# Moving layer three's general pass behind the first two edge groups, and adding a block's two half sums in one instruction

## The chip, the cores and the metric

The kernel runs on one core of one Trainium2 chip. The metric is device time in microseconds (us) of one execution. TensorE (PE) multiplies, VectorE (DVE) and ScalarE (ACT) work elementwise, GpSimd (POOL) here mostly issues gathers (indirect DMAs, which fetch one row of a table for each partition), and SyncE (SP) issues plain DMAs. The engines run side by side, each through its own queue in the order of the program, and wait for each other by semaphores.

## The reference

Three graph layers on 6250 nodes with 128 features and E = 106250 edges, sorted by `dst`. The change lies in the last one alone:

```python
h_edge = jnp.concatenate([x[src], x[dst]], axis=-1)
m_ij = jax.nn.relu(h_edge @ W_interact + b_interact)
m_i = jax.ops.segment_sum(m_ij, src, num_segments=x.shape[0])
m_i = m_i / jnp.asarray(math.sqrt(AVG_DEGREE), dtype=x.dtype)
out = x + jax.nn.relu((x + m_i) @ W_update + b_update)
```

## The kernel before

Layers one and two take the time up to 874 us, where the first product of layer three (L1400) starts. Between them the kernel also sorts the edges by their source, for layer three.

Layer three starts with two products for each node, kept as tables: `a` (the part of `x[src]`, in SBUF as `a_kept`) and `b` (the part of `x[dst]` with the bias, stored to DRAM as `b_rows`). PE makes them in ten chunks (L1400); VectorE adds the bias to b (`b_part`, L2090 and L2093), GpSimd makes the low half of the b tiles that stay in SBUF (L892), and SyncE stores b to `b_rows` (L720).

Then come 50 blocks of 125 source nodes. The sorted edges of a block lie in 18 tiles of 128 edge slots, worked in six groups of three tiles, so there are 300 groups, `gi` from 0 to 299. For a group:

- VectorE makes one-hot matrices that pick rows (`prepare`, L2151, three groups ahead, one instruction for each tile whose b rows are picked by a product; for a block's first group also L2143, which makes those of all 18 tiles for the a rows; for two groups in six also `source_hot`, L2170).
- PE picks the a rows, and for 9 of the 18 tiles the b rows, into a PSUM bank (`edge_sum`, L1434 and L1443).
- For the other 9 tiles of a block GpSimd fetches the b rows from `b_rows` (`fetch`, L901, one gather for a tile, into a ring of nine group buffers that the program calls cells, cell_hi and cell_lo). A buffer is free again when VectorE has added it (semaphore `e_full`), nine groups earlier.
- VectorE adds the gathered rows in PSUM (`add_rows`, L2182), ScalarE takes the relu (L1120), VectorE makes its low half (`low_term`, L2190), and PE sums by source node (`source_sum`, L1454).

At a block's end the high and the low half of the sum lie side by side in PSUM, [125, 2 x 128]. `whole_sum` on VectorE copies the first half to SBUF (L2198) and then adds the second to it (L2200), and `turn_sum` on PE transposes the result (L1466). `whole_sum` for block b - 1 stands in group 4 of block b, behind that group's `prepare`, and directly ahead of `add_rows` of group 5.

The sort reserves a fixed number of slots for each block. A general pass takes care of inputs for which that isn't enough: in that case it goes over all edges tile by tile, in a loop whose trip count is in `trips`. For these inputs the trip counts are one, and the one trip adds zero. It still runs once: VectorE makes two node numbers (`g_node`, L2113, and `g_src`, L2114), GpSimd gathers one row of a and one of b (L918), VectorE adds, clips and scales them (L2117 to L2119), makes a one-hot (L2124), PE multiplies (L1416), and VectorE adds the result to `hT` (L2129). In VectorE's queue and in PE's it stands ahead of all 50 blocks. In GpSimd's it stands behind `fetch(0)` and `fetch(1)`, and GpSimd waits there for the store of `a_rows` (SP, L725) and for `g_idx`.

Of the kernel before, what the change touches and what calls it, by code (L numbers as in the profile page):

```python
# [6 lines left out]
def gnn_kernel(nc, x, src, dst, W_l0, W_r0, b0, W_l1, W_r1, b1, W_int, b_int, W_upd, b_upd, out):  # L7
# [5 lines left out]
    ALU = mybir.AluOpType  # L13
# [169 lines left out]
    with ctx:  # L183
# [404 lines left out]
        SOON = 2  # L588
        BUILT = 10
# [538 lines left out]
        def _(pe):  # L1128
# [283 lines left out]
            n_t, n_b = trips_of(pe)  # L1412
            with pe.Fori(0, n_t) as T:
                with pe.Fori(0, n_b) as b:
                    pe.wait_ge(g_onehot, T * NB + b + 1)
                    t.matmul(ps[:, 6, 0:BN], g_msg, g_hot, start=True, stop=True).then_inc(g_sum, 1)  # L1416
# [30 lines left out]
            def source_sum(gi):  # L1447
# [3 lines left out]
                if g == 0 and b > 1:  # L1451
                    pe.wait_ge(e_whole, 2 * (b - 1))
# [6 lines left out]
            def turn_sum(b):  # L1459
                pe.wait_ge(e_whole, 2 * b + 2)  # L1460
                if b:
                    pe.wait_ge(e_added, b)
                updated = sum(last < b for last in LAST_BLOCK)
                if updated:
                    pe.wait_ge(o_biased, updated)
                t.transpose(ps[:, 7, 2 * P:2 * P + BN], block_sum[0:BN, :], ident[0:BN, 0:BN]).then_inc(e_turned, 1)  # L1466
# [11 lines left out]
            for gi in range(NGR):  # L1478
# [3 lines left out]
                edge_sum(gi)  # L1482
                if g == 2 and b > 1:
                    turn_sum(b - 2)
# [11 lines left out]
        def _(dve):  # L1496
# [611 lines left out]
            n_t, n_b = trips_of(dve)  # L2108
            GENERAL = 3
            with dve.Fori(0, n_t) as T:  # L2110
                chain, n = chained(g_step, T * GENERAL)
                one = pairs[:, bass.ds(T + 1, 1), :].rearrange("p a k -> p (a k)")
                v.tensor_scalar(g_node[:, :], one, gate[:, 3:4], None, ALU.min).then_inc(g_idx, 1)  # L2113
                v.tensor_scalar(g_src[:, :], one[:, 0:1], 1.0, None, ALU.mult).then_inc(g_next, 1)  # L2114
                for k in range(2):
                    dve.wait_ge(g_rows[k], T * 16 + 16)
                chain(v.tensor_tensor(out=g_msg, in0=g_a, in1=g_b, op=ALU.add))  # L2117
                chain(v.tensor_scalar(g_msg, g_msg, 0.0, None, ALU.max))
                chain(v.tensor_scalar(g_msg, g_msg, gate[:, 1:2], None, ALU.mult))  # L2119
                assert n[0] == GENERAL  # L2120
                dve.sem_inc(s_past[1], 1)
                with dve.Fori(0, n_b) as b:
                    dve.wait_ge(g_next, T * (NB + 1) + b + 1)
                    v.tensor_scalar(g_hot, iota_w[:, 0:BN], g_src[:, 0:1], None, ALU.is_equal).then_inc(g_onehot, 1)  # L2124
                    dve.wait_ge(g_onehot, T * NB + b + 1)
                    v.tensor_scalar(g_src[:, :], g_src[:, :], -float(BN), None, ALU.add).then_inc(g_next, 1)
                    dve.wait_ge(g_sum, T * NB + b + 1)
                    to = hT[:, bass.ds(b * BN, BN)]
                    v.scalar_tensor_tensor(out=to, in0=ps[:, 6, 0:BN], scalar=settle[:, 0:1], in1=to,  # L2129
                                           op0=ALU.mult, op1=ALU.add).then_inc(g_added, 1)  # L2130
                    dve.wait_ge(g_added, T * NB + b + 1)
# [62 lines left out]
            def whole_sum(b):  # L2194
                dve.wait_ge(e_psum, (b + 1) * GB)
                if b:
                    dve.wait_ge(e_turned, b)
                v.tensor_copy(block_sum[0:BN, :], ps[0:BN, 4 + b % 2, 0:D]).then_inc(e_whole, 1)  # L2198
                dve.wait_ge(e_whole, 2 * b + 1)
                v.tensor_tensor(out=block_sum[0:BN, :], in0=block_sum[0:BN, :], in1=ps[0:BN, 4 + b % 2, D:2 * D],  # L2200
                                op=ALU.add).then_inc(e_whole, 1)
# [21 lines left out]
            AHEAD = 3  # L2223
# [4 lines left out]
            for gi in range(NGR):  # L2228
# [45 lines left out]
```

## Time and profile before

| | |
|---|---|
| median of three runs | 1581.64 us (1581.3 to 1582.77) |
| the profiled execution | 1582.7 us, its span 1580.9 us |
| busy in the span: PE, VectorE, ScalarE, GpSimd | 1343.8, 1323.1, 874.6, 968.7 us |
| from the first gather of layer three to the end of the span | 918.16 to 1580.9 us |
| gathers of layer three | 450 in L901, 2 in L918 |

The span runs from the first to the last instruction on the core; the time of an execution is a little more. Line numbers are those of the kernel before. A group of rows names line, engine, operation, and what was written from what. "x3" at a row's end is the number of instructions merged in it.

### The profile page before, as it was taken

How to read it: one execution, taken by the hardware profiler on the slowest of the kernel's cores; microseconds unless marked ns; L12 is line 12 of the kernel's file. 1: busy time of each engine (PE TensorE's matmuls, PEld its weight loads, DVE VectorE, ACT ScalarE, POOL GpSimd, SP SyncE). 2: the span in 40 equal slices, each digit the busy share in tenths (PEclk: the TensorE clock that was granted, in tenths of full speed). 3: DMA queues.
4: the chain of work that ended last, by engine and by line, in shares of the span. 5: the costliest groups of instructions: out<-in, count | busy, mean ns of one | idle time of the engine just before them, and what ended most of it. 6: DMA issues, size and time to landing. Idle time of an engine off the chain costs nothing.

```text
span 1580.9 us, 38635 instructions
## 1 busy us (share of the span) xinstructions
PE 1343.8 (85%) x14762; PEld 1138.4 (72%) x14762; DVE 1323.1 (84%) x3131; ACT 874.6 (55%) x1635; POOL 968.7 (61%) x940
## 2 busy tenths in 40 slices
PE   1623888999999988999998859989899999998987
PEld 1311566777777766777776759989898988888886
DVE  7968887999999845767776769989898988998987
ACT  2643676878778930110001637767666766666764
POOL 5263804777771007677750277777777787777775
PEclk9955899999999999999999879999999999999998
DMA  3003644656464238899984234444444444444442
GB/s 118 1 1 98 225 198 142 222 181 245 156 254 144 84 101 283 283 311 306 302 278 154 58 86 131 125 124 123 115 124 114 123 121 114 121 116 123 124 113 74
DMA packets 121777, 241.56 MB, mean 153 GB/s; under 512 B 20184, under 2 KB 74601, under 8 KB 121594
## 3 DMA queue, kind: packets, MB, share of 16 engines
q1 hardware_dynamic: 95179, 187.74, 35.3%
q0 software_dynamic: 24832, 50.78, 13.0%
q8 instruction: 118, 1.93, 0.5%
q10 hardware_dynamic: 1584, 0.59, 0.1%
q14 instruction: 64, 0.52, 0.1%
HBM read 169.09 MB, written 73.14 MB: 153 GB/s over the span
## 4 chain that ended last, share of the span: by engine, by line
PE 34%; DVE 29%; POOL 13%; DMA 9%; issue 9%; SPq 4%; DVEq 1%; ACT 1%; POOLq 0%
PE ps L1238 13%; POOL cells L901 6%; PE ps L1220 5%; DVE hot L1782 4%; PE ps L1443 4%; POOL cell_lo L901 4%; DMA cells<-b_rows,work 4%; POOL cell_hi L901 3%; PE ps L1209 3%; DMA cell_hi<-b_rows,work 3%; SPq L643 2%; DVE room L2151 2%; PE ps L1278 2%; DVE keys L1908 2%; DVE keys L1907 2%
## 5 line engine op out<-in xcount | busy, mean ns | idle before, releaser
L990 ACT ACTIVATE slab<-ps 128x980 f16<-128x980 f32 x256 | 321.6, 1277 | 116.9 <-PE ps L1209 102.2
L901 POOL DMA_INDIRECT cells<-b_rows,work x236 | 271.0, 1148 | 73.7 <-issue 65.5
L1443 PE MATMUL ps<-slab,room 125*128 125x128 f16 x3538 | 236.7, 221 | 20.2 <-DVE room L2151 19.8
L1220 PE MATMUL ps<-slab,room 128*128 128x320 f16 x1568 | 252.2, 301 | 0.1
L1443 PEld LDWEIGHTS ps<-slab,room 125*128 125x128 f16 x3538 | 208.1, 98 | 29.7 <-DVE room L2151 29.6
L1434 PE MATMUL ps<-inv,hot 125*128 125x128 f16 x1800 | 225.2, 221 | 3.7 <-DVE hot L2143 3.6
L1238 PE MATMUL ps<-slab,room 128*128 128x320 f16 x1568 | 227.3, 301 | 0.0
L1209 PE MATMUL ps<-hot 128*128 128x245 bf16 x1024 | 161.8, 283 | 48.7 <-DVE hot L1782 38.0
L865 POOL DMA_INDIRECT hot<-t_rows,pairs x160 | 165.5, 1034 | 55.6 <-issue 48.2
L1238 PEld LDWEIGHTS ps<-slab,room 128*128 128x128 f16 x1568 | 153.2, 98 | 59.8 <-issue 2.7
L1099 ACT ACTIVATE lnw<-iota_w,keys 128x126 f32<-128x126 f32 x600 | 193.9, 389 | 0.0
L1220 PEld LDWEIGHTS ps<-slab,room 128*128 128x128 f16 x1568 | 153.4, 98 | 47.8 <-issue 1.0
L1443 PE MATMUL ps<-slab 125*128 125x128 f16 x2676 | 181.7, 221 | 6.0 <-DVE slab L2151 5.7
L1782 DVE TENSOR_TENSOR hot<-iota_hi,cell_hi 128x984 bf16<-128x984 bf16 x256 | 170.2, 665 | 0.0
L1209 PEld LDWEIGHTS ps<-hot 128*128 128x128 bf16 x1024 | 108.1, 116 | 85.7 <-DVE hot L1782 51.7
L1443 PEld LDWEIGHTS ps<-slab 125*128 125x128 f16 x2676 | 158.3, 98 | 10.4 <-DVE slab L2151 9.8
L865 POOL DMA_INDIRECT tslot<-t_rows,pairs x80 | 95.1, 1189 | 98.8 <-PE ps L1278 67.1
L1434 PEld LDWEIGHTS ps<-inv,hot 125*128 125x128 f16 x1800 | 144.2, 98 | 10.6 <-DVE hot L2143 3.7
L901 POOL DMA_INDIRECT cell_lo<-b_rows,work x115 | 126.4, 1099 | 35.0 <-issue 31.7
L1907 DVE TENSOR_TENSOR keys<-keys 128x256 f32<-128x256 f32 (+1 forms) x212 | 111.9, 528 | 37.2 <-ACT keys L973 21.7
L1120 ACT ACTIVATE slab<-ps 128x384 f16<-128x384 f32 x200 | 95.8, 479 | 77.4 <-DVE ps L2182 74.5
L901 POOL DMA_INDIRECT cell_hi<-b_rows,work x99 | 113.4, 1145 | 30.2 <-issue 26.8
(367 smaller groups left out, 2413.2 us busy)
## 6 DMA issues: line engine op xcount, KB each, us to landing
slabs_d<-slab SPq DMA_DIRECT2D x14, 3920.0 KB, 13.7
slab<-slabs_d SPq DMA_DIRECT2D x98, 560.0 KB, 5.2
hot<-lane_d SPq DMA_DIRECT2D x50, 576.0 KB
inv<-inv_row SPq DMA_DIRECT2D x32, 160.0 KB, 6.5
keys<-up_d SPq DMA_DIRECT2D x25, 160.0 KB
room<-up_d SPq DMA_DIRECT2D x25, 160.0 KB
cells<-b_rows,work POOLq DMA_INDIRECT x236
t_rows<-room SPq DMA_DIRECT2D x1, 3200.0 KB, 13.7
```

What stands on the lines that cost most here:

```text
L865: p.indirect_dma_start(tail_rows[L][i % RT[L]], None, t_rows[L], bass.IndirectOffsetOnAxis(ap=pairs[:, t, 0:1], axis=0)).then_inc(e_gath[a ...
L901: p.indirect_dma_start(rows_g[gi % RS][:, j, :], None, b_rows, bass.IndirectOffsetOnAxis(ap=node_t[:, t:t + 1], axis=0)).then_inc(e_gath[g ...
L990: a.activation(slab[par][:, :, u * UB * BW:(u + 1) * UB * BW].rearrange("p h (k d) -> p k h d", k=UB), psum_unit(u).rearrange("p k (h d) - ...
L1099: last = a.activation(far[:, j, :], iota_w[:, 0:BE], ACT.Square, bias=lane_g[:, gi * GT + j:gi * GT + j + 1])
L1120: a.activation(msg[gi % 3][:, :, 0, :], ps[:, gi % 4, 0:GW].rearrange("p (j f) -> p j f", j=GT), ACT.Relu).then_inc(e_msg, 1)
L1209: last = t.matmul(to[:, k, :], lo[:, :, k], hi[:, k, 0:HB], start=True, stop=True)
L1220: last = t.matmul(ps[:, 4 + s % 2, 0:SC], table[:, h, term, :], slab[s % 2][:, h, :], start=k == 0, stop=k == HI * HALVES - 1)
L1238: last = t.matmul(ps[:, 4 + q % 2, 0:SC], table[:, h, term, :], slab[q % 2][:, h, :], start=k == 0, stop=k == HI * HALVES - 1)
L1434: last = t.matmul(to, lanes_of, a_terms[0:BN, b % 2, k, :], start=k == 0, stop=not picked and k == HALVES - 1)
L1443: last = t.matmul(to, end_hot[g // 3][0:BN, u:u + P], bt[0:BN, bt_at(tile, w), k, :], start=False, stop=w == w1 - 1 and k == HALVES - 1)
L1782: v.tensor_tensor(out=hot[:, u % 4, P * UB:(P + HB + 1) * UB].rearrange("p (k w t) -> p k w t", k=UB, t=2), in0=iota_hi[:, :].rearrange("p ...
L1907: v.tensor_tensor(out=new[0], in0=old[0], in1=old[1], op=ALU.max if down else ALU.min)
```

## The change

It makes two edits. The general pass keeps its place in GpSimd's and SyncE's queues. In VectorE's and PE's it moves into the loop over groups: on VectorE into gi = 1 (`GENERAL_AT`), behind `prepare(4)`; on PE behind `edge_sum(4)` (`GENERAL_AT + AHEAD`). The two node numbers of its first trip are made where the pass stood (`general_pair`), and those of the next trip at a trip's end. And `whole_sum` is one `tensor_reduce` over the two halves, which reads them with a step of 128 elements between the two addends.

```diff
@@ PE
-            n_t, n_b = trips_of(pe)
-            with pe.Fori(0, n_t) as T:
...
+            def general_edges():
+                n_t, n_b = trips_of(pe)
...
-                    pe.wait_ge(e_whole, 2 * (b - 1))
+                    pe.wait_ge(e_whole, b - 1)
...
-                pe.wait_ge(e_whole, 2 * b + 2)
+                pe.wait_ge(e_whole, b + 1)
...
                 edge_sum(gi)
+                if gi == GENERAL_AT + AHEAD:
+                    general_edges()
@@ VectorE
-            n_t, n_b = trips_of(dve)
-            GENERAL = 3
-            with dve.Fori(0, n_t) as T:
-                chain, n = chained(g_step, T * GENERAL)
-                one = pairs[:, bass.ds(T + 1, 1), :].rearrange("p a k -> p (a k)")
+            def general_pair(at):
+                one = pairs[:, at, :].rearrange("p a k -> p (a k)")
                 v.tensor_scalar(g_node[:, :], one, gate[:, 3:4], None, ALU.min).then_inc(g_idx, 1)
                 v.tensor_scalar(g_src[:, :], one[:, 0:1], 1.0, None, ALU.mult).then_inc(g_next, 1)
...
+            general_pair(slice(1, 2))
+
+            def general_edges():
+                n_t, n_b = trips_of(dve)
+                GENERAL = 3
+                with dve.Fori(0, n_t) as T:
+                    chain, n = chained(g_step, T * GENERAL)
+                    for k in range(2):
+                        dve.wait_ge(g_rows[k], T * 16 + 16)
+                    chain(v.tensor_tensor(out=g_msg, in0=g_a, in1=g_b, op=ALU.add))
...
+                    general_pair(bass.ds(T + 2, 1))
...
-                v.tensor_copy(block_sum[0:BN, :], ps[0:BN, 4 + b % 2, 0:D]).then_inc(e_whole, 1)
-                dve.wait_ge(e_whole, 2 * b + 1)
-                v.tensor_tensor(out=block_sum[0:BN, :], in0=block_sum[0:BN, :], in1=ps[0:BN, 4 + b % 2, D:2 * D],
-                                op=ALU.add).then_inc(e_whole, 1)
+                v.tensor_reduce(out=block_sum[0:BN, :], in_=ps[0:BN, 4 + b % 2, 0:2 * D].rearrange("p (k f) -> p f k", k=2),
+                                op=ALU.add, axis=AX.X).then_inc(e_whole, 1)
...
+                if gi == GENERAL_AT:
+                    general_edges()
```

In the order of VectorE's instructions the place is where the b part ends and the blocks start. Before, the pass (L2113 to L2129, with the loops' own steps) comes first, then the first block's preparation:

```order
L2113 TENSOR_SCALAR g_node<-pairs,gate 128x2
L2114 TENSOR_SCALAR g_src<-pairs 128x1
L2116 ISA
L2117 TENSOR_TENSOR scaled<-inv 128x128
...
L2129 SCALAR_TENSOR_TENSOR hT<-ps,settle,hT 128x125
...
L2160 TENSOR_TENSOR inv<-room,inv 125x128
L2143 TENSOR_SCALAR hot<-hot,lane_c 125x2304
```

After, line numbers are 10 or 11 higher. VectorE reaches the first block's preparation straight from the two node numbers, and the pass follows the preparation of the fifth group:

```order
L2115 TENSOR_SCALAR g_node<-pairs,gate 128x2
L2116 TENSOR_SCALAR g_src<-pairs 128x1
L2171 TENSOR_TENSOR inv<-room,inv 125x128
L2154 TENSOR_SCALAR hot<-hot,lane_c 125x2304
...
L2162 TENSOR_TENSOR slab<-keys,down_c 125x896
L505 TENSOR_LOAD trips
L505 ISA x2
...
L2127 TENSOR_TENSOR scaled<-inv 128x128
...
L2139 SCALAR_TENSOR_TENSOR hT<-ps,settle,hT 128x125
```

The gathered rows aren't waited for ahead of the first block any more. On PE the pass's product stood between the b part and the first group; after, it stands behind the picks of the fifth group (L1437 and L1446), and the loads of the trip counts stand there too:

```order
L1457 MATMUL ps<-slab,tslot 126x256 x3
L1437 MATMUL ps<-inv,hot 128x128 x2
L1446 MATMUL ps<-slab 128x128 x14
L1437 MATMUL ps<-inv,hot 128x128 x4
L505 TENSOR_LOAD trips
...
L1419 MATMUL ps<-scaled 128x125
```

GpSimd's, SyncE's and ScalarE's instructions and their order are the same in both kernels.

## Rows read from the trace of the kernel before

**Rows 1.** The page, part 4: shares of the chain that ended last, by engine

```profile
PE 34%; DVE 29%; POOL 13%; DMA 9%; issue 9%; SPq 4%; DVEq 1%; ACT 1%; POOLq 0%
```

**Rows 2.** Timeline of VectorE: start us, us, instruction, [idle before <-releaser]

```profile
914.77 1.32 DVE L2113 TENSOR_SCALAR g_node<-pairs,gate 128x2 int32 x1 [0.18 <-issue]
...
924.87 0.29 DVE L2117 TENSOR_TENSOR scaled<-inv 128x128 f32<-128x128 f32 x1 [8.74 <-DMA inv<-b_rows,g_node]
...
928.75 0.29 DVE L2160 TENSOR_TENSOR inv<-room,inv 125x128 f16<-125x128 f32 x1 [0.46 <-DVE hT L2129]
928.96 1.00 DVE L2143 TENSOR_SCALAR hot<-hot,lane_c 125x2304 f16<-125x2304 f16 x1
...
933.30 0.30 DVE L2182 TENSOR_TENSOR ps<-ps,cells 128x128 f32<-128x128 f32 x1 [0.82 <-PE ps L1434]
```

**Rows 3.** Timeline of TensorE

```profile
926.98 0.79 PE L1416 MATMUL ps<-scaled 128*128 128x125 f32 x2 [13.98 <-DVE scaled L2124]
```

**Rows 4.** Timeline of GpSimd

```profile
918.16 0.96 POOL L901 DMA_INDIRECT cells<-b_rows,work  x1 [2.11 <-DMA b_rows<-cells]
...
920.93 0.94 POOL L918 DMA_INDIRECT inv<-a_rows,g_node  x1 [0.56 <-issue]
...
923.43 0.94 POOL L901 DMA_INDIRECT cells<-b_rows,work  x1 [0.30 <-issue]
...
1567.62 0.94 POOL L901 DMA_INDIRECT cells<-b_rows,work  x1 [0.30 <-issue]
```

**Rows 5.** Waits of GpSimd, 917 to 1581 us: total us, times, longest

```profile
POOL cells L901 <- issue: 65.5, 215, 0.3
...
POOL cells L901 <- DVE ps L2182: 6.1, 20, 0.3
```

**Rows 6.** Waits of VectorE: first row 930 to 1000 us, the others 1000 to 1575 us

```profile
DVE ps L2182 <- PE ps L1434: 2.3, 2, 1.5
...
DVE ps L2182 <- DMA cells<-b_rows,work: 20.2, 23, 2.3
DVE ps L2182 <- DMA cell_hi<-b_rows,work: 19.8, 15, 3.6
DVE ps L2182 <- DMA cell_lo<-b_rows,work: 8.6, 8, 2.6
```

**Rows 7.** Stretches, L901 alone: length, POOL busy (x gathers), TensorE's granted clock, DMA

```profile
918.10:932.70 14.60, 9.08 (x9) 0.50 0.23 49
932.70:1007.20 74.50, 58.05 (x54) 0.98 0.46 121
1007.20:1478.20 471.00, 372.31 (x324) 0.99 0.44 120
1478.20:1556.20 78.00, 61.48 (x54) 0.98 0.44 120
```

**Rows 8.** Timelines of GpSimd (two rows) and VectorE (five) around one whole_sum

```profile
1230.52 1.56 POOL L901 DMA_INDIRECT cells<-b_rows,work  x1 [0.30 <-issue]
1232.39 0.94 POOL L901 DMA_INDIRECT cells<-b_rows,work  x1 [0.30 <-issue]
...
1230.12 1.15 DVE L2151 TENSOR_TENSOR room<-keys,up_c 125x896 f16<-125x896 f16 x2
1231.18 0.28 DVE L2198 COPY scaled<-ps 125x128 f32<-125x128 f32 x1
...
1231.71 0.42 DVE L2182 TENSOR_TENSOR ps<-ps,cell_lo 128x256 f32<-128x256 f32 x1
1232.04 0.55 DVE L2190 SCALAR_TENSOR_TENSOR work<-ps,work 128x384 f16<-128x384 f32 x1
1232.51 0.75 DVE L2151 TENSOR_TENSOR room<-keys,up_c 125x1152 f16<-125x1152 f16 x1
```

**Rows 9.** Timeline of VectorE: a dense reduce, its successor, a copy written with a step

```profile
53.72 0.59 DVE L1656 TENSOR_REDUCE slab<-slab 128x52 f32<-128x416 f32 x1
54.22 0.58 DVE L1653 SCALAR_TENSOR_TENSOR slab<-slab 128x416 f32<-128x416 f32 x1
...
17.35 0.86 DVE L1534 COPY slab<-ps 128x416 f32<-128x416 f32 x1
```

**Rows 10.** Timeline of VectorE: its last addition of gathered rows

```profile
1570.17 0.43 DVE L2182 TENSOR_TENSOR ps<-ps,cells 128x256 f32<-128x256 f32 x1 [0.52 <-DMA cells<-b_rows,work]
```

More of the change, by code:

```diff
@@ L588, in gnn_kernel @@
         SOON = 2
+        AHEAD = 3
+        GENERAL_AT = 1
         BUILT = 10
@@ L1411, in _ @@
                     norm_transpose(NS_[1], c + 2)
-            n_t, n_b = trips_of(pe)
-            with pe.Fori(0, n_t) as T:
-                with pe.Fori(0, n_b) as b:
-                    pe.wait_ge(g_onehot, T * NB + b + 1)
-                    t.matmul(ps[:, 6, 0:BN], g_msg, g_hot, start=True, stop=True).then_inc(g_sum, 1)
+            def general_edges():
+                n_t, n_b = trips_of(pe)
+                with pe.Fori(0, n_t) as T:
+                    with pe.Fori(0, n_b) as b:
+                        pe.wait_ge(g_onehot, T * NB + b + 1)
+                        t.matmul(ps[:, 6, 0:BN], g_msg, g_hot, start=True, stop=True).then_inc(g_sum, 1)
             pe.wait_ge(f_aok, NC)
@@ L2114, in _ @@
                 v.tensor_scalar(g_src[:, :], one[:, 0:1], 1.0, None, ALU.mult).then_inc(g_next, 1)
[L2115 to L2131, printed above, removed]
+            general_pair(slice(1, 2))
@@ new lines, in general_edges @@
+            def general_edges():
[6 more added lines that the diff above has]
+                    chain(v.tensor_tensor(out=g_msg, in0=g_a, in1=g_b, op=ALU.add))
+                    chain(v.tensor_scalar(g_msg, g_msg, 0.0, None, ALU.max))
+                    chain(v.tensor_scalar(g_msg, g_msg, gate[:, 1:2], None, ALU.mult))
+                    assert n[0] == GENERAL
+                    dve.sem_inc(s_past[1], 1)
+                    with dve.Fori(0, n_b) as b:
+                        dve.wait_ge(g_next, T * (NB + 1) + b + 1)
+                        v.tensor_scalar(g_hot, iota_w[:, 0:BN], g_src[:, 0:1], None, ALU.is_equal).then_inc(g_onehot, 1)
+                        dve.wait_ge(g_onehot, T * NB + b + 1)
+                        v.tensor_scalar(g_src[:, :], g_src[:, :], -float(BN), None, ALU.add).then_inc(g_next, 1)
+                        dve.wait_ge(g_sum, T * NB + b + 1)
+                        to = hT[:, bass.ds(b * BN, BN)]
+                        v.scalar_tensor_tensor(out=to, in0=ps[:, 6, 0:BN], scalar=settle[:, 0:1], in1=to,
+                                               op0=ALU.mult, op1=ALU.add).then_inc(g_added, 1)
+                        dve.wait_ge(g_added, T * NB + b + 1)
+                    general_pair(bass.ds(T + 2, 1))
@@ L2221, in residual @@
                                        ).then_inc(o_sum, 1)
-            AHEAD = 3
             split_lo(0)
```

## The prediction

> **What bounds the kernel now.** I first looked at the chain that ended last [rows 1]. It names PE and VectorE for two thirds of the span, and inside the change's place it also runs over the general pass: VectorE's idle 8.74 us ahead of L2117 [rows 2] and PE's 13.98 us ahead of L1416 [rows 3]. That would make the move worth some 12 us. So I asked a second question: does anything later make up for a late start of VectorE and PE? For this the reader should look at GpSimd, which no share of busy time points to.
>
> GpSimd's timeline of layer three starts at 918.16 us, released by the store of the b rows, and its last gather starts at 1567.62 [rows 4]. Its waits [rows 5] are all of one size: 0.3 us at most, whether the view puts them down to "issue" or to VectorE's L2182 (20 times, 6.1 us, so 0.3 each). So 0.3 us is the time between two gathers, and a buffer of the ring was always free before GpSimd came to it. GpSimd issues 452 gathers, and never waits for VectorE or PE.
>
> VectorE's waits complete the picture [rows 6]. Up to 1000 us it never waits for a gather, only 2.3 us for PE. It starts 12 us late and works off rows that have long landed. From 1000 us on it waits for gathers 46 times (23 + 15 + 8), 48.6 us in all, and its last addition at 1570.17 us waits for one too [rows 10]. From 1000 us to the end layer three goes at the pace of GpSimd's queue. The chain view can't show this: it follows the small gaps of GpSimd to VectorE because L2182 is what the semaphore names.
>
> What sets GpSimd's pace is how long a gather takes. Per gather it was busy 9.08/9 = 1.01 us up to 932.7, while VectorE stood still for most of the time; then 58.05/54 = 1.075; then 372.31/324 = 1.149; and 61.48/54 = 1.139 in blocks 43 to 48 [rows 7]. An undisturbed one takes 0.94. [Rows 8] show a disturbed one: the gather from 1230.52 takes 1.56 and ends at 1232.08, which is 0.81 us after a pair of L2151 ended (1231.27). I found this 0.81 again behind most long gathers: one that begins while VectorE is in an instruction with two SBUF inputs (L2151) ends 0.81 us after that instruction. The next gather begins at 1232.39, 0.12 us ahead of the next L2151 (1232.51), and takes 0.94. The Trainium skill (GPSIMD Engine Reference, Key points) says that GpSimd shares its SBUF interfaces with VectorE and contends with its instructions in a two-port mode or with two SBUF inputs; the trace agrees.
>
> **The move, step by step.** Removed: VectorE's wait. It can go on when L2113 ends, 914.77 + 1.32 = 916.1, and I take 916.5 for the start of L2160 in place of 928.75, 12 us earlier, and PE with it. Added: the pass now stands between groups 1 and 2. On VectorE that is 924.87 to 928.75, 3.9 us, plus a second pair of node numbers (under 0.5) and a wait for PE, which comes to its product only behind five groups and two loads of trip counts. I take 5 to 7 us for all of it. Behind it wait `add_rows(2)`, ScalarE's relu of that group, and PE's sum of group 1. VectorE still comes to block 1 about 6 us earlier than before.
>
> What does GpSimd make of it? Its first gather waits for the store of b, which is issued by the same b part as before. Its general gathers start at 920.93, when `g_idx` is long there in both kernels. So the queue starts at 918.16 and has the same 452 gathers: the gain at the start is worth nothing at the end. The 12 us turn into waits of VectorE for gathers, from block 1 on rather than from 1000 us.
>
> A small loss is left. VectorE's L2143 and L2151 of the first groups now run beside the first nine gathers. If these take 1.139 us as late blocks' do, in place of 1.01, that is 9 x 0.13 = 1.2 us. In blocks 1 to 6 VectorE ran free of the gathers before, and they took 1.075; in the mirrored blocks 43 to 48, with the same L2151 work but VectorE waiting for gathers, 1.139. If the waiting is the cause, 54 x 0.064 = 3.5 us more. The bounds are 0 and 4.7 us; I take the first term whole and a third of the second, 2.4 us. I put it below the middle as the difference may have other causes.
>
> **The reduce.** One `whole_sum` costs VectorE 0.53 us before (1231.18 to 1231.71 [rows 8]). The trace has no reduce that reads with a step. From below: the dense reduce of 416 elements took 0.50 us to its successor [rows 9]; 128 elements fewer cost 0.13 us (L2182: 0.43 us for 256 [rows 8], 0.30 for 128 [rows 2]), so 256 elements take 0.50 - 0.16 = 0.34. From above: the copy of 416 elements that writes with a step took 0.86 against 0.59 for the dense reduce [rows 9], 0.27 more, or 0.17 for 256 elements: 0.51. The reduce reads every element 128 away from the last, which is nearer to the stepped copy, so I take 0.48.
>
> The Trainium skill (Vector Engine (DVE) Microarchitecture Reference, Measured stream behaviour) gives 1.73 ns per element where a source hops at every element, and some 75 ns fixed; that would be 0.52 us, by an estimate from that page. It measured SBUF; no row here shows a stepped read of PSUM.
>
> So the edit saves VectorE 0.05 us, at most 0.19, per block. VectorE has 48.6 us of waits for gathers, which swallow it: nothing in the middle. At the end of block 49 no gather is left, and there it counts once: 0.05 to 0.2 us.
>
> **The sum.** Against the profiled execution: 1582.7 + 2.4 - 0.1 = 1585.0. That execution is 1.1 us above the median, so for a median I say 1583.9. Its own range is 1581 to 1587 (the two bounds, and up to 1 us for the phase).
>
> **The rivals.**
>
> *The start counts (faster).* If the chain view is right, the end moves with VectorE's start: 12 us less 6 for the pass, so 6 us, and up to 50 x 0.19 = 9.5 us for the reduce. 1567 to 1576, say 1573. For it: PE and VectorE have 34% and 29% of the chain and are over 80% busy. Against it: GpSimd's longest gap [rows 5] and the waits at the end [rows 6, 10]. Chance 0.10.
>
> *The reduce moves VectorE onto the gathers (slower).* If the reduce costs 0.34, all behind it comes 0.19 us earlier. In [rows 8] the L2151 of 1232.51 would start at 1232.32, ahead of the gather of 1232.39. It would end at 1233.07 and the gather 0.81 later, at 1233.88 in place of 1233.33: 0.55 us lost in GpSimd's queue, which has no slack. This can happen in the blocks where `add_rows` of group 5 doesn't wait. By the 46 waits these are at least 4 of 50, and 50 at most; with 27, 15 us. A gather that ends later meets other instructions, and VectorE then waits more often and starts its L2151 later, so I count half: 8 us, 1590. It decides where the reduce costs less than about 0.53 - 0.12 = 0.41 us. For it is the dense reduce; against it the stepped copy. The page's rule on shared interfaces is what speaks for this rival, that on hopping sources against it. Chance 0.27.
>
> *The phase goes the other way (faster).* Gathers and L2151 keep a pattern from block to block, and any shift can also make it better. Were 350 gathers to take 1.13 in place of 1.149 us, that gives 6.6 us: 1575. Nothing in the rows speaks for a side. Chance 0.08.
>
> *The pass inside the loop stalls GpSimd.* VectorE stands for up to 7 us ahead of `add_rows(2)`. GpSimd needs that group's buffer only for group 11, 14 gathers behind 923.43 [rows 4], at 0.94 + 0.30 each 17 us later, at 940.8; VectorE is there at about 931. It would take a stall of 17 us. With the other unknowns I give it 0.05, at no change.
>
> **How the numbers follow.** 0.2% is 3.2 us, about what a measurement of this kernel can tell from no change: 1578.5 to 1584.8. The forecast has 0.50. Of it 0.38 lies within 0.2%, and 0.12 above (its bound is 4.7 us plus phase). The slower rival has 0.24 above and 0.03 within, the two faster ones 0.17 below and 0.01 within, the rest 0.05 within. Faster 0.17, same 0.47, slower 0.36. The range leaves out the larger part of the first rival and the upper end of the second: 1577 to 1592.
>
> **What the profile after would show.** Right: GpSimd's first gather near 918.2 and no gap over 0.3 us; VectorE's first L2182 near 921 in place of 933.3; VectorE waiting for gathers before 1000 us too, its total rising from 48.6 to some 55 to 60; the gathers of the first nine taking more than 1.01 us; the last gather starting 1 to 5 us later than 1567.62. For the reduce: 0.48 us to the next instruction. Wrong: a last gather before 1566, which would mean that gathers are disturbed less; a reduce at 0.34 with means per gather over 1.17; or a gap of GpSimd behind `e_full`.

## The result: 0.8% slower

| | before | after |
|---|---|---|
| median | 1581.64 us (1581.3 to 1585.96, 5 runs) | 1596.07 us (1590.46 to 1600.54, 5 runs) |
| the profiled execution, its span | 1582.7, 1580.9 us | 1597.12, 1595.3 us |
| busy: PE, VectorE, ScalarE, GpSimd | 1343.8, 1323.1, 874.6, 968.7 us | 1348.1, 1314.1, 875.1, 998.6 us |
| L901 (L903 after): first start, last start | 918.16, 1567.62 us | 916.10, 1581.58 us |

The ratio on record is 1.0081, 95% interval 1.0053 to 1.0109. VectorE has 9 us less work than before and GpSimd is busy for 30 us more, though its 940 instructions are the same. Half of these 30 us lie ahead of 905 us, where the two kernels do the same (449.4 us before and 464.4 after; the kernel before in a second profile, e0, has 457.6): that is scatter of the earlier layers. The other half lies in layer three, and only that is explained here. Lines of after are two higher for GpSimd, two or three for PE, and 9 to 11 for VectorE (L903 for L901, L2162 for L2151, L2193 for L2182).

The page of after, part 4 (before: [rows 1]). POOL's share went from 13 to 23%:

```profile
PE 30%; POOL 23%; DVE 23%; issue 10%; DMA 9%; SPq 4%; DVEq 1%; ACT 1%; POOLq 0%
```

The timeline of VectorE after, at the start of layer three (before: [rows 2]):

```profile
914.53 0.29 DVE L2171 TENSOR_TENSOR inv<-room,inv 125x128 f16<-125x128 f32 x1 [1.80 <-ACT inv L1110]
...
918.91 0.30 DVE L2193 TENSOR_TENSOR ps<-ps,cells 128x128 f32<-128x128 f32 x1 [0.82 <-PE ps L1437]
...
921.82 0.61 DVE L2162 TENSOR_TENSOR slab<-keys,down_c 125x896 f16<-125x896 f16 x1
923.95 0.32 DVE L2127 TENSOR_TENSOR scaled<-inv 128x128 f32<-128x128 f32 x1 [1.52 <-DMA inv<-b_rows,g_node]
...
927.04 0.35 DVE L2139 SCALAR_TENSOR_TENSOR hT<-ps,settle,hT 128x125 f32 x1 [1.20 <-PE ps L1419]
...
928.01 0.43 DVE L2193 TENSOR_TENSOR ps<-ps,cells 128x256 f32<-128x256 f32 x1
```

VectorE adds its first gathered rows at 918.91 us in place of 933.30. The pass costs it 5.6 us, from 922.43 (the end of L2162) to 928.01; 1.52 of these it waits for the pass's own gathered rows and 1.20 for PE.

The stretches of GpSimd's L903 after (before: [rows 7]): length, busy (x gathers), TensorE's granted clock, DMA.

```profile
918.10:932.70 14.60, 9.36 (x10) 0.85 0.26 55
932.70:1007.20 74.50, 58.96 (x52) 0.97 0.43 117
1007.20:1478.20 471.00, 374.08 (x319) 1.00 0.44 118
```

In the same 471 us GpSimd gets through 319 gathers in place of 324, as each takes 1.173 us in place of 1.149 (374.08/319 and 372.31/324). Over all 450, the mean is 1.171 us in place of 1.135. The row that matters most is the smallest: behind its first gather, GpSimd's waits still have 0.3 us as their longest (before: [rows 5]).

```profile
POOL cells L903 <- issue: 67.6, 222, 0.3
...
POOL cells L903 <- DVE ps L2193: 4.0, 13, 0.3
```

So its queue never stands, after as before. From the start of the first gather to that of the last it takes 665.5 us in place of 649.5 (1581.58 - 916.10 and 1567.62 - 918.16), and these 16 us are longer gathers. VectorE's waits for them went from 48.6 us to 8.8 us ahead of 1000 us and 71.3 us behind it (before: [rows 6]):

```profile
DVE ps L2193 <- DMA cell_lo<-b_rows,work: 25.2, 17, 3.5
DVE ps L2193 <- DMA cells<-b_rows,work: 24.5, 23, 2.7
DVE ps L2193 <- DMA cell_hi<-b_rows,work: 21.6, 18, 3.9
```

The reduce in all 50 blocks, its line in the view by source line (duration in ns: least, median, most):

```profile
L2209 DVE TENSOR_REDUCE scaled<-ps x50: 410/420/434, 944.6 to 1586.7; 125x128 f32<-125x256 f32 x50
```

And one place where it acts, GpSimd's and VectorE's timelines of after in a block in which VectorE doesn't wait (before: [rows 8]):

```profile
1223.39 1.56 POOL L903 DMA_INDIRECT cell_hi<-b_rows,work  x1 [0.31 <-issue]
1225.26 1.75 POOL L903 DMA_INDIRECT cell_hi<-b_rows,work  x1 [0.30 <-issue]
...
1222.98 1.16 DVE L2162 TENSOR_TENSOR room<-room,up_c 125x896 f16<-125x896 f16 x2
1224.05 0.42 DVE L2209 TENSOR_REDUCE scaled<-ps 125x128 f32<-125x256 f32 x1
1224.38 0.43 DVE L2193 TENSOR_TENSOR ps<-ps,cells 128x256 f32<-128x256 f32 x1
1224.71 0.55 DVE L2201 SCALAR_TENSOR_TENSOR work<-ps,work 128x384 f16<-128x384 f32 x1
1225.17 0.76 DVE L2162 TENSOR_TENSOR room<-room,up_c 125x1152 f16<-125x1152 f16 x1
1225.84 0.36 DVE L2181 TENSOR_TENSOR tslot<-iota_hi,blk 128x378 f16<-128x378 bf16 x1
```

The next instruction starts 0.33 us behind the reduce (1224.38 - 1224.05). The picks of group 5 (L2162 at 1225.17) now begin 0.09 us ahead of a gather (1225.26) in place of 0.12 us behind one, and that gather takes 1.75 us in place of 0.94. It ends at 1227.01, 0.81 us behind the end of L2181 (1226.20), which follows L2162 without a gap and has two SBUF inputs too.

To see how much this is, I put each gather's time over 0.94 us on the VectorE instruction in progress 0.1 us behind its start. Before, 7 gathers lost 2.0 us to the picks of group 5; after, 31 lost 17.3 us. All gathers together lost 88 us before and 104 after. That is the 16 us by which the queue got longer. The other groups' gains and losses about cancel: 5.4 us more on L2143, 4.0 less on the picks of group 0. "Picks of group 5" are those that VectorE makes in its turn of group 5, behind that group's `add_rows`. Why the picks of group 5 moved, and whether this or the move of the pass makes the time, is what the experiments ask.

### The profile page after: what moved, and what is told of

It reads as the page before. It is cut to its first block, busy times and chain, and to the rows that moved or that the text cites. A ratio compares the mean times of both kernels' runs of the same rounds, so it can differ in the third digit from the quotient of the medians.

```text
span 1595.3 us, 38587 instructions
## 1 busy us (share of the span) xinstructions
PE 1348.1 (85%) x14762; PEld 1136.7 (71%) x14762; DVE 1314.1 (82%) x3083; ACT 875.1 (55%) x1635; POOL 998.6 (63%) x940
## 4 chain that ended last, share of the span: by engine, by line
PE 30%; POOL 23%; DVE 23%; issue 10%; DMA 9%; SPq 4%; DVEq 1%; ACT 1%; POOLq 0%
PE ps L1240 13%; POOL cells L903 12%; POOL cell_lo L903 6%; PE ps L1222 5%; POOL cell_hi L903 5%; DVE hot L1787 4%; DMA cells<-b_rows,work 3%; PE ps L1211 3%; SPq L645 2%; PE ps L1280 2%; DMA cell_hi<-b_rows,work 2%; DVE keys L1913 2%; DVE keys L1912 2%; DVE hot L1782 2%; DVE slab L1658 1%
## 5 line engine op out<-in xcount | busy, mean ns | idle before, releaser
L903 POOL DMA_INDIRECT cells<-b_rows,work x236 | 273.9, 1160 | 73.7 <-issue 67.6
L1446 PE MATMUL ps<-slab,room 125*128 125x128 f16 x3538 | 237.0, 221 | 23.6 <-DVE room L2162 23.4
L1446 PEld LDWEIGHTS ps<-slab,room 125*128 125x128 f16 x3538 | 207.9, 98 | 34.8 <-DVE room L2162 34.1
L1437 PE MATMUL ps<-inv,hot 125*128 125x128 f16 x1800 | 225.1, 221 | 8.0 <-DVE hot L2154 7.9
L1446 PE MATMUL ps<-slab 125*128 125x128 f16 x2676 | 181.0, 220 | 6.4 <-DVE slab L2162 5.9
L867 POOL DMA_INDIRECT tslot<-t_rows,pairs x80 | 113.8, 1423 | 96.6 <-PE ps L1280 64.0
L1446 PEld LDWEIGHTS ps<-slab 125*128 125x128 f16 x2676 | 156.8, 98 | 12.4 <-DVE slab L2162 11.2
L903 POOL DMA_INDIRECT cell_lo<-b_rows,work x115 | 138.1, 1200 | 35.1 <-issue 34.1
L1437 PEld LDWEIGHTS ps<-inv,hot 125*128 125x128 f16 x1800 | 143.7, 98 | 16.2 <-DVE hot L2154 7.3
L903 POOL DMA_INDIRECT cell_hi<-b_rows,work x99 | 115.2, 1163 | 30.2 <-issue 27.7
```

Of the source, the lines that this page charges most:

```text
L867: p.indirect_dma_start(tail_rows[L][i % RT[L]], None, t_rows[L], bass.IndirectOffsetOnAxis(ap=pairs[:, t, 0:1], axis=0)).then_inc(e_gath[a ...
L903: p.indirect_dma_start(rows_g[gi % RS][:, j, :], None, b_rows, bass.IndirectOffsetOnAxis(ap=node_t[:, t:t + 1], axis=0)).then_inc(e_gath[g ...
L1437: last = t.matmul(to, lanes_of, a_terms[0:BN, b % 2, k, :], start=k == 0, stop=not picked and k == HALVES - 1)
L1446: last = t.matmul(to, end_hot[g // 3][0:BN, u:u + P], bt[0:BN, bt_at(tile, w), k, :], start=False, stop=w == w1 - 1 and k == HALVES - 1)
```

## The experiments

Ratios are to the kernel before on the same chip, with their 95% intervals. Three chips were used: one for e0 to e6 and e9, one for e7, e8, e10 and e12 to e15, and one for e16, so a comparison across these sets goes by the ratios. "Gather loss" is what all gathers of a profiled execution took over 0.94 us each, put on VectorE's instructions as above. It stands for that one execution: e3's was its fastest (1588.4 us, its median is 1593.71), e13's its slowest (1571.38, median 1565.34), and e0's 4.6 us below its median.

| kernel | ratio | gather loss, us | of it on group 5's picks | on L2143 |
|---|---|---|---|---|
| before / after | 1 / 1.0081 | 88 / 104 | 2.0 / 17.3 | 13 / 19 |
| e0 before, again | 0.9996 [0.9972, 1.0020] | 86 | 2.2 | 16 |
| e1 the move alone | 1.0006 [0.9983, 1.0029] | 95 | 4.3 | 19 |
| e2 the reduce alone | 1.0103 [1.0070, 1.0135] | 110 | 17.5 | 22 |
| e3 after + idle copy, 0.53 us | 1.0058 [1.0038, 1.0078] | 95 | 3.2 | 21 |
| e4 reduce + idle copy, 0.53 us | 1.0045 [1.0023, 1.0067] | 102 | 4.0 | 26 |
| e10 reduce + idle copy, 0.41 us | 1.0121 [1.0097, 1.0146] | 111 | 19.3 | 22 |
| e14 reduce + idle copy, 0.47 us | 1.0021 [0.9997, 1.0044] | 98 | 3.2 | 25 |
| e15 reduce + idle copy, 0.52 us | 1.0049 [1.0024, 1.0075] | 102 | 2.5 | 25 |
| e16 reduce, wait, idle copy, 0.53 us | 1.0000 [0.9979, 1.0020] | 88 | 2.1 | 17 |
| e12 copy, add, idle copy, 0.60 us | 0.9979 [0.9958, 1.0001] | 89 | 2.9 | 12 |
| e7 half sums ahead of group 4's picks | 0.9881 [0.9860, 0.9902] | 75 | 4.6 | 18 |
| e13 e7 with the move | 0.9874 [0.9852, 0.9895] | 79 | 5.4 | 25 |
| e8 e7 with the reduce | 1.0135 [1.0100, 1.0170] | 113 | 11.6 | 20 |

The losses carry the times. In all 16 profiled executions with 450 gathers the span is the time from the first gather's start to the last one's and 927 to 932 us more (before 649.5 + 931.4, after 665.5 + 929.8, e7 636.4 + 927.0, e8 674.4 + 930.3). Only the length of that queue tells the kernels apart.

### One part at a time (e1, e2)

e1 is the kernel after with the copy and the addition put back; e2 is the kernel before with the reduce. The edit that e1 undoes and e2 makes:

```diff
-                v.tensor_copy(block_sum[0:BN, :], ps[0:BN, 4 + b % 2, 0:D]).then_inc(e_whole, 1)
-                dve.wait_ge(e_whole, 2 * b + 1)
-                v.tensor_tensor(out=block_sum[0:BN, :], in0=block_sum[0:BN, :], in1=ps[0:BN, 4 + b % 2, D:2 * D],
-                                op=ALU.add).then_inc(e_whole, 1)
+                v.tensor_reduce(out=block_sum[0:BN, :], in_=ps[0:BN, 4 + b % 2, 0:2 * D].rearrange("p (k f) -> p f k", k=2),
+                                op=ALU.add, axis=AX.X).then_inc(e_whole, 1)
```

> The move alone; a block's half sums are copied and added by two instructions as before. Theory (the reduce slides VectorE's next picks onto a gather, the move changes nothing but early waits): within 0.3% of before, 1580 to 1587, the gathers of blocks 7 to 42 at 1.15 us as before, and behind the two instructions the picks start 0.12 us behind a gather. Rival (the move is what costs, by coupling VectorE to the gathers from the start): 1590 or more. Rival (the start counts): under 1577.

> The reduce alone; the general pass stays ahead of the blocks. Theory: the whole loss, 1590 to 1600; the reduce takes 0.34 us to its successor, and in the blocks where group 5 doesn't wait for its rows the picks start about 0.08 us ahead of a gather, which then takes 1.76 us in place of 0.94. Rival (the move is what costs): 1580 to 1584.

The move is worth nothing that can be measured, 1.0006; the reduce alone makes it 1.0103 times as long, as much as both edits together within the intervals. The place of [rows 8] in e2, GpSimd and VectorE:

```profile
1232.03 1.49 POOL L901 DMA_INDIRECT cell_hi<-b_rows,work  x1 [0.30 <-issue]
...
1230.83 0.41 DVE L2198 TENSOR_REDUCE scaled<-ps 125x128 f32<-125x256 f32 x1
1231.16 0.42 DVE L2182 TENSOR_TENSOR ps<-ps,cells 128x256 f32<-128x256 f32 x1
...
1231.95 0.75 DVE L2151 TENSOR_TENSOR room<-room,up_c 125x1152 f16<-125x1152 f16 x1
```

The picks begin 0.08 us ahead of the gather, which ends 0.82 us behind them. (In most blocks of e2 it ends 0.81 us behind L2170, which follows the picks, and loses 0.82 us in place of 0.55.) So the reduce does it. Whether by being short or by something else in it is the next question.

### Is it the length? (e3, e4, e10, e14)

Each has the reduce and behind it an idle copy out of PSUM, whose result nothing reads: 125 elements (e3 on the kernel after, e4 on the kernel before), 8 in e10, 69 in e14. e14's edit:

```diff
                 v.tensor_reduce(out=block_sum[0:BN, :], in_=ps[0:BN, 4 + b % 2, 0:2 * D].rearrange("p (k f) -> p f k", k=2),
-                                op=ALU.add, axis=AX.X).then_inc(e_whole, 1)
+                                op=ALU.add, axis=AX.X)
+                v.tensor_copy(scaled[0:BN, D:D + 69], ps[0:BN, 4 + b % 2, 0:69]).then_inc(e_whole, 1)
```

> The changed kernel with an idle copy of 125 PSUM elements behind each block's reduce, which does no work that is needed and takes up the 0.19 us that the reduce saved. Theory (only the moment counts at which VectorE's next instructions start): back to 1580 to 1587 though VectorE does more work, picks again 0.1 us behind a gather. Rival (the reduce itself disturbs gathers, or the move costs): it stays at 1590 to 1600.

> The kernel before with the reduce and the same idle copy, the general pass in its old place. Theory: within 0.3% of before, 1579 to 1585. Rival (the reduce itself disturbs gathers): as slow as the reduce alone.

> The kernel before with the reduce, followed by an idle copy of 8 PSUM elements (about 0.08 us, no needed work), 0.42 us in all. Theory: the picks of group 5 start at 0.00 to 0.03 us behind the gather, where before no gather was held: what gathers lose to group 5's picks falls from 17.5 to under 6 us, and the time lies at 1588 to 1597, like the reduce with the long idle copy. Rival (the reduce itself disturbs): over 1599, like the reduce alone.

> The kernel before with the half sums added by the reduce, followed by an idle copy of 69 elements out of PSUM that nothing reads. Reduce 0.334 us and copy about 0.14 us to the next start, so 0.475 us together: the length that the prediction gave to the reduce. Theory (the first pick of group 5 must start at least some 0.05 us behind the start of the gather): it starts about 0.07 us behind, so the loss on picks of group 5 stays at the 2 to 4 us of the kernel before, and the time at 0.999 to 1.006 times before's. Rival (any start earlier than before's is held): gathers lose 15 us on picks of group 5 and the time is 1.010 to 1.013 times before's.

From the start of the reduce to that of `add_rows` it is 0.334 us in e2, 0.407 in e10, 0.471 in e14 and 0.528 in e4, where nothing waits. The picks of group 5 begin 0.08 us ahead of the gather in e2, within 0.01 us of it in e10, 0.07 behind it in e14, and 0.11 in e4. The loss on them is 17.5, 19.3, 3.2 and 4.0 us. There is an edge. The picks of all groups in the 15 traces with all gathers and all picks show where it lies. Of 153 that began 0.04 to 0.10 us ahead of a gather, every one held it; of 443 that began 0.02 to 0.18 us behind one, none did; in between, 32 of 75 did. e10 stands in the band between, where the picks of group 5 still held most gathers, and e14 behind it:

```profile
1227.63 1.83 POOL L901 DMA_INDIRECT cell_hi<-b_rows,work  x1 [0.30 <-issue]
...
1226.42 0.42 DVE L2198 TENSOR_REDUCE scaled<-ps 125x128 f32<-125x256 f32 x1
1226.75 0.16 DVE L2200 COPY scaled<-ps 125x8 f32<-125x8 f32 x1
...
1227.62 0.75 DVE L2151 TENSOR_TENSOR room<-room,up_c 125x1152 f16<-125x1152 f16 x1
```

```profile
1219.40 0.94 POOL L901 DMA_INDIRECT cell_hi<-b_rows,work  x1 [0.31 <-DVE ps L2182]
...
1218.21 0.41 DVE L2198 TENSOR_REDUCE scaled<-ps 125x128 f32<-125x256 f32 x1
1218.54 0.21 DVE L2200 COPY scaled<-ps 125x69 f32<-125x69 f32 x1
...
1219.47 0.74 DVE L2151 TENSOR_TENSOR room<-room,up_c 125x1152 f16<-125x1152 f16 x1
```

0.06 us more of idle work, 50 times, moves the ratio from 1.0121 to 1.0021. I had expected e10 to be like e4, at 1588 to 1597 us with under 6 us lost on group 5's picks; it was as slow as e2, 1604.61 us with 19.3 lost. Its recorded rival, that the reduce itself disturbs the gathers, gave this time (over 1599) too; e14 and e16, which keep the reduce and lose 3.2 and 2.1 us there, rule it out. This is a step and not a slope. e14 has the length that the prediction gave to the reduce, and its loss on group 5's picks is close to that of the kernel before.

e3 and e4 give back the loss on group 5, but not the whole time, and both missed what I expected of them (the time of before): 1.0058 and 1.0045 stand. The table shows another loss there, on L2143 (the one-hot of a block's first group), 21 and 26 us for 13 to 16 before.

### What is left of it (e15, e12, e16)

e15 is e14 with 112 elements. e12 has the old copy and addition and an idle copy of 8 elements behind them. e16 has the reduce with the structure of the old pair:

```diff
-                v.tensor_copy(block_sum[0:BN, :], ps[0:BN, 4 + b % 2, 0:D]).then_inc(e_whole, 1)
+                v.tensor_reduce(out=block_sum[0:BN, :], in_=ps[0:BN, 4 + b % 2, 0:2 * D].rearrange("p (k f) -> p f k", k=2),
+                                op=ALU.add, axis=AX.X).then_inc(e_whole, 1)
                 dve.wait_ge(e_whole, 2 * b + 1)
-                v.tensor_tensor(out=block_sum[0:BN, :], in0=block_sum[0:BN, :], in1=ps[0:BN, 4 + b % 2, D:2 * D],
-                                op=ALU.add).then_inc(e_whole, 1)
+                v.tensor_copy(scaled[0:BN, D:D + 8], ps[0:BN, 4 + b % 2, 0:8]).then_inc(e_whole, 1)
```

> The kernel before with the half sums added by the reduce, followed by an idle copy of 112 elements that nothing reads: 0.334 + 0.19 = 0.525 us to the next start, within a few ns of the old pair. If the few ns by which the longer idle copy differed from the pair made its 0.45%, the time is 0.998 to 1.002 times before's. If something of the reduce itself costs time, 1.003 to 1.006, as with the longer copy.

> The kernel before with its copy and addition, followed by an idle copy of 8 elements that nothing reads: 0.60 us to the next start in place of 0.53, no reduce. It leaves the first pick of group 5 some 0.19 us behind the gather's start, with no loss there. If only the group-5 loss and VectorE's own time count: 0.999 to 1.001 times before's. If any shift of VectorE's later work by tens of ns moves losses between the groups: 0.3 to 0.6% away from 1 on either side, with the changes in the losses on L2143 and on the picks of groups 0, 1 and 3.

> The kernel before with the reduce in the place of the copy, VectorE waiting for its end as it did for the copy's, and then an idle copy of 8 elements that nothing reads in the place of the addition. 0.42 us for the reduce, 0.03 for the wait and 0.07 for the copy make 0.52 us, the pair's length, and PE waits for the second instruction as before. If the missing wait or the signals made the 0.5% of the kernels with reduce and long idle copy, the time is 0.998 to 1.002 times before's, and L2143 holds gathers for 12 to 18 us. If it is the reduce itself: 1.003 to 1.006, and 21 to 26 us on L2143.

e16 is the clean one. It has the reduce in all 50 blocks, and 1.0000. Its place of [rows 8]:

```profile
1232.91 0.94 POOL L901 DMA_INDIRECT cells<-b_rows,work  x1 [0.30 <-DVE ps L2182]
...
1231.71 0.41 DVE L2198 TENSOR_REDUCE scaled<-ps 125x128 f32<-125x256 f32 x1
1232.16 0.17 DVE L2201 COPY scaled<-ps 125x8 f32<-125x8 f32 x1
1232.24 0.43 DVE L2182 TENSOR_TENSOR ps<-ps,cell_lo 128x256 f32<-128x256 f32 x1
...
1233.04 0.75 DVE L2151 TENSOR_TENSOR room<-keys,up_c 125x1152 f16<-125x1152 f16 x1
```

The picks begin 0.13 us behind the gather, which isn't held. So the reduce as such costs nothing that can be measured (0.2% either way): made as long as the pair, with the pair's wait, it gives the pair's time. e12 shows that lengthening the sum by 0.07 us doesn't cost anything either.

e15 is 1.0049 all the same. It is 12 ns shorter than e16 up to `add_rows` (0.516 and 0.528 us) and lacks the wait between the two instructions; e4, at the same 0.528 as e16, has 1.0045. In the profiled executions a gather that begins in L2143 loses over 1.3 us 14 times in e15 and in e4, 8 times in e16, 6 and 9 times in the two of before, and 5 times in e12. At 1.47 us for most of these, 6 more are 9 us. That fits the 0.5%, but e14 has 15 of them with 1.0021, and e13 has 15 and is 1.3% faster than before. What in a sum without the wait leads more blocks to that place half a block later wasn't found, and e16 ran on another chip than e15 and e4. This part stays open.

These longest holds aren't L2143's alone. In the kernel before, two picks follow it without a gap, and the gather ends 0.82 us behind them (1230.22 and 1229.40):

```profile
1227.80 2.42 POOL L901 DMA_INDIRECT cells<-b_rows,work  x1 [0.30 <-issue]
...
1227.52 0.81 DVE L2143 TENSOR_SCALAR hot<-hot,lane_c 125x2304 f16<-125x2304 f16 x1
1228.25 1.15 DVE L2151 TENSOR_TENSOR room<-keys,up_c 125x640 f16<-125x640 f16 x2
```

By itself L2143 holds a gather too, but for less. In e9 below, in a block without picks:

```profile
1356.11 1.50 POOL L901 DMA_INDIRECT cells<-b_rows,work  x1 [0.30 <-issue]
...
1355.99 0.81 DVE L2143 TENSOR_SCALAR hot<-hot,lane_c 125x2304 f16<-125x2304 f16 x1
```

### Is GpSimd's queue the bound? (e5, e6, e9)

These leave out work, so their outputs aren't the reference's. e5 and e6 gather one tile in place of two in the groups that have two, 300 gathers in place of 450, so that the second tile's b rows are stale; e5 is otherwise the kernel before, e6 is e1. e9 makes the picks of b rows (L2151) in only nine of the 50 blocks; in the others it writes two elements for each of them. (The expectation says ten blocks; the edit has nine.)

```diff
-                for j, tile in enumerate(GROUPS[g][1]):
+                for j, tile in enumerate(GROUPS[g][1][:1]):
```
```diff
...
+                    if b not in (0, 2, 5, 9, 14, 36, 41, 45, 48):
+                        last = v.memset(end_hot[h][0:BN, at * P:at * P + 2], 0.0)
+                        continue
```

> The kernel before, but of a group's two gathers only the first is issued (300 in place of 450; the second tile's rows are then stale, so their part of the sum is left out). Theory (GpSimd's queue sets the pace): GpSimd is no longer the bound, VectorE waits for hardly any gather, and the time falls to what VectorE and PE need, 50 blocks of 11.1 us from 933 on, some 1500. Rival (VectorE and PE are the bound anyway): a few us below the kernel before.

> The same 300 gathers (half of the two-tile groups' rows left out), and the general pass moved as in the change, half sums by two instructions. Theory (the early start is real, only swallowed by GpSimd's queue): 5 to 8 us faster than the same kernel without the move. Rival (the move gives nothing at all): within 2 us of it.

> The kernel before, but L2151 works only in ten of the 50 blocks; in the others the one-hots of an earlier block stay (a memset of two columns takes its place), so the rows of b picked by products are wrong, and PE and GpSimd have the same work. Theory (VectorE's instructions with two SBUF inputs lengthen the gathers): a gather takes under 1.02 us in place of 1.135, and the end comes 50 to 70 us earlier, 1515 to 1535. Rival (the length of a gather has other causes, such as DMA): over 1.10 us, less than 20 us earlier.

e5 took 1523.01 us (0.9610 [0.9579, 0.9640]) and e6 1515.88 (0.9561 [0.9529, 0.9592]). The waits of GpSimd in e5 show what changed:

```profile
POOL cells L901 <- DVE ps L2182: 157.6, 161, 2.3
POOL cell_lo L901 <- DVE ps L2182: 61.8, 61, 1.6
POOL cell_hi L901 <- DVE ps L2182: 55.5, 61, 1.7
```

GpSimd now waits for free buffers, 275 us in all, and VectorE waits for no gather from 1000 us on. Under that bound the move is worth 7.1 us (e6 against e5, four runs of each, 1513.0 to 1517.5 and 1521.9 to 1525.4 us), the 12 us of the start less the pass's 5.6 within a us. With all 450 gathers it was worth nothing. So the start was swallowed because GpSimd's queue is the bound.

e9 took 1517.91 us (0.9583 [0.9549, 0.9617]) with all its gathers. Its stretch from 1007.20 us on:

```profile
1007.20:1478.20 471.00, 360.21 (x364) 1.00 0.50 134
```

0.99 us for a gather in place of 1.149. VectorE's picks are most of what makes gathers longer, and without nearly all of them the kernel takes 4.2% less with the same number of gathers.

### Where to put the sum (e7, e8, e13) and the control (e0)

If only the place relative to the gathers counts, then the sum's 0.53 us can do good elsewhere. Before, 47 gathers lost 24.4 us to the picks of group 4, ahead of the sum. e7 puts the sum ahead of them:

```diff
+                if g == 4 and b:
+                    whole_sum(b - 1)
                 if gi + AHEAD < NGR:
                     prepare(gi + AHEAD)
                     source_hot(gi + AHEAD)
...
-                if g == 4 and b:
-                    whole_sum(b - 1)
```

> The kernel before with the two half-sum instructions moved ahead of the same group's picks (L2151), nothing else. VectorE does the same work. Theory (a gather starts 1.11 us behind the end of the picks that held the last one, and is held if VectorE is by then in the next picks): the picks of group 4 start at 0.33 + 0.46 + 0.53 - 0.08 = 1.24 us in place of 0.71, so 0.12 us behind the gather's start in place of 0.4 ahead; the 24 us that gathers lose to group 4's picks fall to under 8, the picks of group 5 then meet the gather's end, and the kernel is faster by 8 to 25 us. Rival (the total of held gathers is about the same in whatever order): within 0.3%.

> The same order, and the half sums by one reduce, which is 0.19 us shorter. Theory: the picks of group 4 then start 0.07 us ahead of the gather in place of 0.12 behind, and hold it again; slower than the same order with two instructions by 10 us or more, though VectorE has less work. Rival: as fast or faster than with two instructions.

> The move of the general pass, and the two half-sum instructions ahead of group 4's picks. Theory: the gain of the new order holds with the move too, 8 to 25 us faster than before; if it brings GpSimd's queue below what VectorE and PE need in some blocks, the early start shows as 1 to 5 us more. Rival: the move's early waits disturb the pattern, and the gain is gone.

> The kernel before once more, for its trace on this chip beside the others. Every theory: the ratio holds one; gathers at 1.13 to 1.15 us. It tells how far one kernel's own pattern of disturbed gathers wanders: if its gathers behind a half sum stay undisturbed (under 5 us in all) while its total wanders by several us, then the few us between the other kernels are such wandering.

e7 took 1565.6 us, 0.9881, faster than both kernels. GpSimd and VectorE in e7:

```profile
1068.90 0.94 POOL L901 DMA_INDIRECT cells<-b_rows,work  x1 [0.30 <-issue]
1070.15 0.95 POOL L901 DMA_INDIRECT cells<-b_rows,work  x1 [0.30 <-issue]
...
1068.50 0.28 DVE L2198 COPY scaled<-ps 125x128 f32<-125x128 f32 x1
1068.81 0.29 DVE L2200 TENSOR_TENSOR scaled<-scaled,ps 125x128 f32<-125x128 f32 x1
1069.01 1.15 DVE L2151 TENSOR_TENSOR room<-keys,up_c 125x896 f16<-125x896 f16 x2
```

The pair of picks at 1069.01 begins 0.11 us behind the gather of 1068.90, which isn't held; in [rows 8], where the same pair began 0.40 us ahead of a gather, that one took 1.56 us. The loss on group 4's picks fell from 24.4 to 1.6 us. e8, the same order with the reduce, is 42 us slower than e7 (1607.34 and 1565.6):

```profile
1234.64 1.35 POOL L901 DMA_INDIRECT cell_hi<-b_rows,work  x1 [0.30 <-issue]
...
1234.24 0.41 DVE L2198 TENSOR_REDUCE scaled<-ps 125x128 f32<-125x256 f32 x1
1234.57 1.14 DVE L2151 TENSOR_TENSOR room<-room,up_c 125x896 f16<-125x896 f16 x2
```

The pair now begins 0.07 us ahead of the gather; the loss on group 4's picks is 31.0 us and that on group 5's 11.6. e13 shows that e7's gain holds with the moved pass (0.9874), and that the pass adds nothing to it. e0, the kernel before run as one of the set, gave 0.9996.

## Why the prediction was wrong

**The bound, and the start: right.** Behind the general gathers the queue of GpSimd has no gap over 0.32 us in any kernel with 450 gathers, the last gather sets the end, and the 12 us of the start are worth nothing (e1), but 7 us once GpSimd isn't the bound (e6 against e5). The pass took 5.6 us, where "5 to 7" was said, with 1.20 us of it waiting for PE; its wait of 1.52 us for its gathered rows wasn't in the sum. GpSimd didn't stall behind it.

**The move's 2.4 us: not shown.** Of the first nine gathers in e1, six took 0.94 or 0.95 us; their mean was 1.02 us, against 1.01 before and not 1.139, so the term of 1.2 us was 0.1. The 54 gathers of blocks 1 to 6 took 1.093 us each in e1 against 1.075 before, 1.0 us in all, where 1.2 was put; but the kernel before in its second profile has 1.069, so this is hardly more than scatter. e1's interval (-2.7 to +4.6 us) holds both 0 and 2.4. The first gather was at 916.10 in after, and at 914.1 to 918.6 over the kernels here without an edit ahead of it, so this is scatter of some 4 us that no step of the sum had.

**The reduce: the step that failed.** It said "nearer to the stepped copy, so I take 0.48", and it was 0.33: the lower bound, worked out as 0.34 from the dense reduce. So the edit took 0.19 us from each block's sum where the sum had 0.05, and that moved the picks of group 5 across the edge. The bound was right, and the choice between the bounds wrong. The stepped copy of [rows 9] writes with a step to SBUF; the reduce reads with a step from PSUM and writes densely, and this had no price: 0.42 us for 256 elements, what L2182 takes for 256 dense ones (0.43). The trace of before had a nearer row that wasn't used: L1538, a reduce of 208 elements out of PSUM, two to each result, took 0.336 us. Its two addends lie side by side, so it gives the operation and the memory, not the step.

The Trainium skill (Vector Engine (DVE) Microarchitecture Reference, Measured stream behaviour) has the 1.73 ns per element, from which the prediction's estimate of 0.52 us came, for an instruction with two sources in SBUF of which one hops. The same section says that a one-source instruction whose reads alternate between two regions 16 KiB apart, and that writes one word for two read, ran at the full read rate. But for the distance (512 B here) that is the reduce's pattern, and the trace agrees, out of PSUM: 0.42 us. So the estimate took the wrong one of that section's cases.

**The rival that came true.** The prediction has it in full: at 0.34 the picks of group 5 start ahead of the gather, which decides below 0.41 us. e10 (0.407) and e14 (0.471) lie on the two sides of this edge. With e14's 0.471 the time is 1.0021 [0.9997, 1.0044], that is 1585 us by the median before, so with a reduce of 0.48 the forecast of 1583.9 would most likely have stood; that e15 and e4, which are longer still, took 0.5% more than before is what no step of it had. The Trainium skill's GPSIMD Engine Reference, Key points, was what spoke for this rival (contention with VectorE's instructions that have two SBUF inputs), and the traces agree: 31 gathers held on the picks of group 5 in after, 7 before. The chance of 0.27 was too low for a term whose value was a choice between two rows, one of which was an instruction of the same kind.

**Its price: half was wrong.** "So I count half: 8 us" rested on held gathers meeting other work and VectorE waiting more. The time was 14 us over before, the loss on group 5's picks 15.3 us more, and all losses together 16 us more. On balance nothing was given back. Two more numbers of it were off, and offset each other. In after VectorE doesn't wait ahead of the picks of group 5 in 20 blocks, not 27, and in 17 of these the picks held a gather. Each of these gathers lost 0.68 to 0.82 us, more than the 0.55 reckoned, because L2181 behind the picks extends the hold. That is 13 us of the 17.3; the rest are smaller losses in other blocks.

The range ended at 1592 because of this half; with the whole 15 us the rival would have stood at 1597, and the median was 1596.07. That these come so close is in part luck, as the two numbers offset each other.

**The views.** The chain of waits was the wrong guide before and says more after: POOL grew from 13 to 23%. What the profile was said to show when the forecast fails, "a reduce at 0.34 with means per gather over 1.17", is what it showed: 0.33, and 1.171 over all gathers.

## What to carry to other kernels

Where the bound is a queue of short instructions whose length depends on what another engine does at that moment, saving work on the other engine can cost time: price the new starting moments, not the busy time. Look in one block for who begins just ahead of whom, find the edge (here between 0.04 us ahead of and 0.02 us behind a gather's start), and ask of each edit to which side it moves the next instructions. The same view finds gains for nothing: one block of work placed elsewhere in the order gave 1.2%. And where two rows bound an unknown cost, take the one of the same operation and memory over the one that only shares an access pattern.

## What the runs showed of the hardware that I had not expected

- A `tensor_reduce` of two addends 128 elements apart in PSUM runs as fast as a dense addition: 0.42 us for 256 elements, 0.33 us to the next start.
- A gather takes 0.94 us, and the next starts 0.30 us later. One that begins while VectorE is in an instruction with two SBUF inputs ends 0.81 us after it (1.75 us in the rows of after, two such instructions in a row). One that begins 0.07 us ahead of such an instruction isn't held at all. L2143, with one tensor input in f16 and a number for each partition, holds gathers too: one took 1.50 us in a block of e9 without picks. With the picks that follow it in the other kernels, gathers lose up to 1.48 us. In the places read here copies, additions and reduces out of PSUM didn't hold a gather that began in them.
- 50 idle copies of 69 elements, work that nothing needs, made the kernel with the reduce alone some 13 us faster (1.0021 for 1.0103, each against before on its own chip). With copies of 8 elements it was 1.0121, on the chip of the 69.
